# An increment on a drain in place of one on the last matmul, in the routing and at both ends of the expert loop

## What is computed

```
x = x + layernorm(attn(layernorm(x)))
x = x + layernorm(ffn(layernorm(x)))

# attn: z = sigmoid(relu([shifted x, x] W_act)) as pairs (re, im), divided by the running
# maximum of |z|, multiplied up along the tokens; the result times W_val, times r ** 4
# ffn:
probs = softmax(x @ gate_w.T)                  # 64 experts
topk_w, topk_idx = top_k(probs, 6)             # weights made to sum to 1
h = silu(x @ experts_w1[e].T)                  # 176 wide
y = h @ experts_w2[e].T                        # weighted sum over a token's 6 experts
out = y_sum + (silu(g) * u) @ shared_down.T    # g, u = split(x @ shared_gate_up.T)
```

## Time and profile before

| what | before |
|---|---|
| timed runs, median (lowest to highest) | 280.43 us (279.81 to 282.03) |
| the profiled execution, from its first instruction to its last | 287.2 us |
| TensorE busy (matmuls) | 236.9 us, 82% |
| VectorE busy | 175.1 us, 61% |
| GpSimd busy | 128.2 us, 45% |
| ScalarE busy | 81.5 us, 28% |
| chain that ended last, by engine | PE 49%, DVE 19%, issue 13%, DMA 6%, "another core or an unknown queue" 4% |

### The profile page before, as it was taken

How to read it: one execution, slowest core, us unless ns; L and a number is a source line. 1 busy time by engine, 2 the same in 40 slices (tenths; PEclk the granted TensorE clock), 3 DMA queues, 4 the chain that set the end, 5 groups by cost and what they waited for, 6 DMA issues and landing times.

```text
span 287.2 us, 4231 instructions
## 1 busy us (share of the span) xinstructions
PE 236.9 (82%) x1382; PEld 178.1 (62%) x1382; DVE 175.1 (61%) x552; ACT 81.5 (28%) x188; POOL 128.2 (45%) x162
## 2 busy tenths in 40 slices
PE   6978939976398884349878898999999989989990
PEld 6534818552153663227666687888888858758880
DVE  4539896989997857261308698753433333443884
ACT  2586631384021145000012222112222411120033
POOL 7008300004776574654767326566565654561000
PEclk9999998999599999576979999999999997999998
DMA  6999999997322232445298999999959732668913
GB/s 225 349 376 371 371 369 421 421 417 308 106 106 84 88 115 83 162 146 164 102 290 291 394 314 344 339 377 340 361 180 350 256 119 75 219 222 271 348 42 110
DMA packets 34615, 72.00 MB, mean 251 GB/s; under 512 B 4576, under 2 KB 24608, under 8 KB 34080
## 3 DMA queue, kind: packets, MB, share of 16 engines
q1 hardware_dynamic: 29024, 55.68, 55.8%
q0 software_dynamic: 5568, 16.03, 14.9%
HBM read 44.89 MB, written 26.80 MB: 250 GB/s over the span
## 4 chain that ended last, share of the span: by engine, by line
PE 49%; DVE 19%; issue 13%; DMA 6%; another core or an unknown queue 4%; SPq 3%; ACT 3%; POOL 2%; ACTq 0%; POOLq 0%; DVEq 0%
PE bank L959 9%; PE bank L933 7%; PE bank L955 5%; PE bank L772 4%; PE bank L943 4%; PE bank L1023 4%; PE bank L976 4%; PE bank L790 4%; DMA early<-x_slots 3%; PE bank L781 3%; DMA x_slots<-rows,slot_i 3%; PE bank L842 2%; DVE stats L1088 2%; SPq L392 2%
## 5 line engine op out<-in xcount | busy, mean ns | idle before, releaser
L615 POOL DMA_INDIRECT y_rows<-zbuf,token_i x66 | 64.2, 973 | 50.8 <-DVE zbuf L1425 35.6
L567 POOL DMA_INDIRECT x_slots<-rows,slot_i x48 | 47.0, 980 | 61.9 <-DVE slot_i L1240 34.9
L1425 DVE COPY zbuf<-bank 128x256 f32<-128x256 f32 x66 | 24.7, 419 | 59.0 <-PE bank L959 45.3
L721 ACT ACTIVATE sgu_sb<-bank 128x256 f32<-128x256 f32 x33 | 12.6, 383 | 111.8 <-remote 56.2
L933 PE MATMUL bank<-work,w_all 128*128 128x128 f32 x256 | 35.9, 292 | 2.9 <-issue 2.1
L933 PEld LDWEIGHTS bank<-work,w_all 128*128 128x128 f32 x256 | 33.5, 207 | 3.7 <-issue 3.6
L959 PE MATMUL bank<-w_all,sgu_sb 128*128 128x256 f32 x128 | 35.3, 412 | 0.0
L976 PE MATMUL bank<-ident,early 128*128 128x128 f32 x128 | 21.1, 294 | 14.7 <-DMA early<-x_slots 12.8
L1409 DVE COPY work<-bank 128x512 f32<-128x512 f32 x33 | 22.5, 684 | 12.9 <-PE bank L976 9.9
L808 PE MATMUL bank<-x2nT,sgu_sb 128*128 128x256 f32 (+3 forms) x72 | 23.9, 481 | 7.4 <-DVE nt L1358 7.4
L959 PEld LDWEIGHTS bank<-w_all,sgu_sb 128*128 128x128 f32 x128 | 23.5, 197 | 10.0 <-issue 7.6
(11 more groups left out here) (218 smaller groups left out, 353.7 us busy)
## 6 DMA issues: line engine op xcount, KB each, us to landing
w_all<-pairs SPq DMA_DIRECT2D x32, 752.0 KB, 8.4
x_slots<-hidT SPq DMA_DIRECT2D x8, 1152.0 KB, 12.4
early<-x_slots SPq DMA_DIRECT2D x64, 144.0 KB
w_all<-y_rows SPq DMA_DIRECT2D x4, 1024.0 KB, 6.4
w_all<-y_rows SPq DMA_DIRECT2D x4, 512.0 KB, 10.4
y_rows<-zbuf,token_i POOLq DMA_INDIRECT x66
x_sb<-x SPq DMA_DIRECT2D x4, 256.0 KB, 3.6
out<-work SPq DMA_DIRECT2D x4, 256.0 KB, 2.1
```

Source lines behind the costliest of these rows:

```text
L567: return pool.indirect_dma_start(x_slots, bass.IndirectOffsetOnAxis(ap=slot_i[:, c, k:k + 1], axis=0), rows[:, c, :], None)
L615: pool.indirect_dma_start(y_rows, bass.IndirectOffsetOnAxis(ap=token_i[:, s % 32:s % 32 + 1].bitcast(U32), axis=0), yS[:, s % 8, :], None) ...
L1425: dve.tensor_copy(yS[:, s % 8, :], y_b[s % 4][:, 0:C]).then_inc(y_done, 1)
```

## The change

A helper issues a drain, an instruction of TensorE's queue that waits until the engine has finished what stands ahead of it, and the drain carries the increment. It takes the place of the increment on the last matmul in the second and third unit's `turn_unit`, `logits` and `rank`, in `product_v` 2 and 3, in `gate_up` 3 to 8, in `counts`, and in `rest`, `output` and `turn_rows` for every t outside the quads. `turn_unit` used to give one increment behind each of its two groups of transposes; for units 1 and 2 it now gives both at its end. Every matmul stays where it is, and no engine waits for another count than before. Inside the quads, and before the second half of the tokens, the last matmul still carries the increment.

```diff
+            def arrived(signal, n=1):
+
+                pe.drain().then_inc(signal, n)
+
...
@@ turn_unit(u), for each of the two groups of transposes
-                    mm.then_inc(x2T_ps, 1)
+                    if u == 0:
+                        mm.then_inc(x2T_ps, 1)
+                if u > 0:
+                    arrived(x2T_ps, KC)
...
@@ product_v(k)
-                mm.then_inc(v_ps, 1)
+                if k < 2:
+                    mm.then_inc(v_ps, 1)
+                else:
+                    arrived(v_ps)
...
@@ logits(u); rank(u) the same with rank_ps
-                mm.then_inc(lg_ps, 1)
+                if u == 0:
+                    mm.then_inc(lg_ps, 1)
+                else:
+                    arrived(lg_ps)
...
@@ gate_up(n)
-                if g == 1:
+                if g == 1 and n < 3:
                     mm.then_inc(gu_ps, 1)
+                elif g == 1:
+                    arrived(gu_ps)
...
@@ counts()
-                mm.then_inc(count_ps, 1)
+                arrived(count_ps)
...
+            def alone(t):
+
+                return not QUADS[0] <= t < QUADS[1]
+
...
@@ rest(t); output(t) and turn_rows(t) the same with y_ps and tx_ps
-                mm.then_inc(h_ps, 1)
+                if alone(t):
+                    arrived(h_ps)
+                else:
+                    mm.then_inc(h_ps, 1)
```

More of the change, by code:

```diff
@@ L822, in rank @@
                               start=False, stop=False)
-                pe.matmul(rank_b[:, E * a:E * z], ones[:], expert8[:, 0:z - a, :].rearrange("p c e -> p (c e)"),
-                          start=False, stop=True).then_inc(rank_ps, 1)
+                mm = pe.matmul(rank_b[:, E * a:E * z], ones[:], expert8[:, 0:z - a, :].rearrange("p c e -> p (c e)"),
+                               start=False, stop=True)
+                if u == 0:
+                    mm.then_inc(rank_ps, 1)
+                else:
+                    arrived(rank_ps)
             def counts():
@@ L830, in counts @@
                 for t in range(NT):
-                    mm = pe.matmul(count_b[:, 0:E], ones[:], mask[:, t, :], start=(t == 0), stop=(t == NT - 1))
-                mm.then_inc(count_ps, 1)
+                    pe.matmul(count_b[:, 0:E], ones[:], mask[:, t, :], start=(t == 0), stop=(t == NT - 1))
+                arrived(count_ps)
             def keep_warm(b, n):
@@ L960, in output @@
                                        weights(2 * t)[:, PW2 + C * i:PW2 + C * i + C], start=False, stop=True)
-                    mm.then_inc(y_ps, 1)
+                    if alone(t):
+                        arrived(y_ps)
+                    else:
+                        mm.then_inc(y_ps, 1)
             def turn_rows(t):
@@ L976, in turn_rows @@
                         mm = pe.transpose(x_b[t % 2][:, at:at + P], src[:, P * k:P * k + P], ident[:])
-                mm.then_inc(tx_ps, 1)
+                if alone(t):
+                    arrived(tx_ps)
+                else:
+                    mm.then_inc(tx_ps, 1)
             pe.wait_ge(rank_read, 3)
```

## The result

The changed kernel takes 292.28 us (median of four, 291.25 to 296.71), the kernel before in the same comparison 281.02 (279.81 to 282.03): a ratio of 1.039 (95% interval 1.033 to 1.045), 11 us slower, and outside the range that was given. Ratios here leave out executions more than 1.5% above the fastest of their kernel; medians hold all. The traced execution of the changed kernel has a span of 289.8 us and took 291.56. In every run the time is 1.7 to 1.8 us above the span, so the execution of before that the rows show, with a span of 287.2, stands for some 289 us. None of the 56 timed executions of before took more than 283.6. The prediction rested on an unusual execution.

A forecast was written before the change was run, and what follows sets the result against it. An engine relay bounds 72 to 164 us, then TensorE sets the pace. A 1.55 us gain up to 142 us, less 0.45 net lost in the last stretch, gave -1.1 us of span and a 279.3 us median; range 274.8 to 286.5.

The forecast's parts named there:

- The gain is 3.72, if the pause is gone: Last stretch, from 224 us: prompt hand-off of `rest(27)` saves 1.98 of waiting and 1.74 of half clock.
- 0.94 and 1.16 in the routing: Routing, 72 to 112 us: gains from prompt hand-offs behind `product_v` (0.94) and the last ranking matmul (1.16).
- the third rival: Whole kernel: late hand-offs belong to the profiled execution alone, so only the drains' price is left, 285.6 us; chance 0.13.
- 0.04 was taken: Behind each drain: TensorE's time to start anew, put at 0.04 us.
- The row of 0.10: Last stretch: TensorE's start behind VectorE's copy, 0.10 us, the nearest profile row for the restart; it includes the increment's way.
- 0.16, 0.25 and 0.26 were forecast: Price in us of one drain behind `rest`, `output` and `turn_rows`: lost overlap, drain's end and restart.
- the cheap rival: Every drain: costs only the lost overlap, 0.07 to 0.17 us, giving 276.2 us in all; chance 0.24.
- the wait for the first rows: Routing: cover for the drains of `gate_up` 4, 5, 7, 8 and `counts`, whose transposes TensorE reaches with time to spare.
- 1.1 was taken as lost: Routing and relay, 72 to 142 us: drains' losses at `turn_unit` (0.1), ahead of `rank(2)` (0.55) and `rest(1)` to `turn_rows(2)` (0.45).
- The 0 that was taken for the drains here: 142 to 164 us: five drains against an earlier freed VectorE, transfers full; 0 net, bounds 0.9 gain and 0.5 loss.
- From there to 224 the hand-offs keep their matmuls: 164 to 224 us: no drains there, TensorE sets the pace, so the earlier gain of 1.55 us is carried through.
- The slower rival: Every drained hand-off: drain ends no earlier than the late increment, nothing gained, 5.3 us lost, 285.6 us; chance 0.18.

The follow-up runs named there:

- tail_waits_ahead: Kernel before with drains from pair 26 on alone, the next step's semaphore waits put ahead of each drain: 288.63 us, ratio 1.025.
- before_again: The kernel before, without an edit, run for a second trace: 278.91 us.
- drain_routing: Kernel before with the 15 drains in the routing alone, none in the expert pairs: 282.80 us, ratio 1.006.
- drain_to_pair5: Kernel before with the 33 drains in the routing and pairs 0 to 5, none from pair 26 on: 285.91 us, ratio 1.016.
- fill7: 7 matmuls that nobody reads put into TensorE's waits for rows: 279.97 us on the kernel before, 285.53 on drain_to_pair5.
- after_again: The changed kernel, without a further edit, run for a second trace: 293.59 us.
- drain_tail: Kernel before with the 19 drains from pair 26 on alone: 290.96 us, ratio 1.039.
- fill7_after: Changed kernel with 7 unread matmuls in TensorE's waits for rows and one more behind the last output: 292.15 us, ratio 1.039.

## Why the prediction was wrong

**The base.** The step that failed first is the one that set the gain: "The gain is 3.72, if the pause is gone", and with it 0.94 and 1.16 in the routing. These were differences within one execution, and a second execution of the same kernel has none of them. Its hand-offs are as prompt with matmuls (0.04, 0.06) as the changed kernel's with drains (0.05, 0.07). That is the third rival, which got 0.13; what it named, a span longer than the median by about as much as the late hand-offs cost, was the sign to go by. The reason given against it, that the time may leave something out at the ends, is refuted by every run, where the time is above the span. With no gain the prediction's own terms come to 5.3 us lost, or 285.6; the rest of the way to 292.28 is terms that were too small. The Trainium skill (PSUM — Partial Sum Buffer, Engine vs sequencer instructions) has it that an instruction's own increment fires at its completion; the second trace agrees, with those 0.04 and 0.06 us, and the first one doesn't (1.71 and 4.98).

**The price of a drain.** The parts were right: the lost overlap (0.07 behind `rest`, 0.16 behind the other two), an end within 0.02 to 0.04 of the last matmul where 0.05 was taken. The restart was mis-sized: 0.04 was taken, 0.21 measured. The row of 0.10 was at hand and set aside as too high. From `output(24)` to the last output stand 17 of the 19 drains; they cost 6.87, 0.40 each, where 0.16, 0.25 and 0.26 were forecast, and the cheap rival 0.07 to 0.17. `rest(26)` stands ahead of `output(24)`, with two drains that the sum left out: its parts (15, 18 and 19) make 52 of the 54, and the missing ones are those of `turn_rows(26)` and `turn_rows(27)`. These three cost 1.21 (12.34 against 11.13), again 0.40 each. The last drain lies in the pause, 0.77. That makes 8.9 in place of 4.2. That most of the restart (0.15) is the waits behind the drain is shown by tail_waits_ahead. The Trainium skill (Perfetto Trace Analysis, Sequencer-only Instruction (DRAIN, etc)) says that the sequencer fetches and decodes the next instruction only after a drain has ended and its increment is pushed; the trace agrees: the wait L978 stands at 231.78, 0.10 behind the end of the drain, with TensorE empty. That the pause behind the last output, where TensorE also reads a register for a branch, grew by 0.77 for the same reason was not tried.

**Routing and relay.** The cost in front of `rank(2)` was sized rightly: from the start of the unit's last transpose to the end of `rank` it takes 4.87 against 4.20 in before_again, 0.67 where 0.55 was taken. It met no gain. The drains that were given a cover, "the wait for the first rows", had it in drain_routing (2.18 of 2.53 taken back). With the drains of pairs 0 to 5 as well, the cover is not always there. Routing and relay together, up to the first y send, lose 0.77 and 4.41 in the changed kernel's two traces, 4.99 in drain_to_pair5, and 3.0 at equal clock (fill7), where 1.1 was taken as lost (0.55 + 0.1 + 0.45). What decides between 0.8 and 5 stays open: the half clock goes with a part of it, but after_again has no more of it than before_again.

**142 to 164 us and the quads.** The place was full: the DMA share is 1.01. The 0 that was taken for the drains here holds: from the first y send to `output(20)` the changed kernel's traces take 71.19 and 71.26, before_again 71.27 (all 17 traces: 70.56 to 73.45). What failed is the next step, "From there to 224 the hand-offs keep their matmuls": the 1.1 to 1.2 that the stage is longer are the three drains between `output(20)` and `output(24)`. That interval is 11.13 in all 9 traces without drains from pair 26 on, and 12.29 to 12.56 in all 8 with them.

**The sum.** In the changed kernel's two traces 12.7 and 13.2 us are lost against before_again: 6.9, 0.8 and 1.2 are the 21 drains from `turn_rows(26)` on, and the rest is 0.8 of routing and relay with 3.1 of half clock at the shared expert in the one, 4.4 of routing and relay in the other. The 8.9 of the 21 drains are shown: both of these traces, drain_tail and fill7_after have them to 0.1. That the clock is lost at all because of the drains is not settled. The half clock at the shared expert stands in 2 of 6 traces that have drains in the last stretch and no fill behind it, and in none of the 9 without such drains. The slower rival, "the drain is as late as the matmul", is refuted: in the changed kernel's trace every drain ends 0.02 to 0.04 us behind the last matmul.

## What to carry to other kernels

Where the traced execution is some per cent longer than the timed runs, a second trace comes before any theory on what the first one shows. A drain in a stream of float32 matmuls without gaps cost 0.40 us each time here, and 0.15 of it was the wait behind it: if a drain must be there, put the next step's waits ahead of it. An increment on the last matmul was as prompt in before_again as one on a drain.

## What was not expected of the hardware

With 18 drains in pairs 0 to 5 one kernel's executions fell into two groups 4 us apart, at a mean granted clock of 0.94 and 0.925; that the drains keep the clock down is a guess that no trace tests. TensorE's increments were up to 7.7 us late in one execution of before (the third y tile ends at 142.71 and is copied from 150.37), and in none of the 16 other traces here; TensorE went on behind VectorE's copies in time. That trace is odd in itself: for 101 of VectorE's 548 increments it holds no semaphore event within 0.15 us of the instruction's end, and no other trace has more than one such. Its timeline has 16 waits ended by "remote", and no other has one. What makes such an execution, and whether taking the profile had a part in it, stays open, and whether drains would have helped in it was not tried, since it could not be called up.
